# SyncE fetches one of the 64 row tiles of a round, row by row

## The reference

```python
f0, f1 = fctp_scalar(x0, x1, node_attr, W_l1_0, W_l1_1, MUL)   # a row of 128 numbers per node
weight = (SILU_NORM * silu(edge_scalars @ (W_fc1 / 8.0))) @ (W_fc2 / 8.0)
g0 = f0[edge_src]                       # 32 numbers of the source's row
g1 = f1[edge_src]                       # 32 x 3 numbers of it
outA = wA * g0 * e0
outB = wB * einsum('euk,ek->eu', g1, e1) / SQRT3
outC = (wC * g0)[..., None] * e1[:, None, :]
outD = wD[..., None] * g1 * e0[..., None]
# mA .. mD: segment sums of these by edge_dst; then small matrices, cos and sin, a layer norm
```

## Time and profile before

| | us |
|---|---|
| median of 3 runs | 7639.68 (7636.81 to 7649.67) |
| the profiled execution | 7641.61 |
| its span | 7639.8 |
| product stage: first to last gather | 3564.9 to 7595.2 |

### The profile page before, as it was taken

The page is one execution under the profiler, slowest core; times in us unless marked ns, Lnnn a source line. Parts: engine busy times, 40 slices in busy tenths (PEclk is TensorE's granted clock), DMA queues, the critical chain, the costliest instruction groups (busy, mean ns, idle before and its releaser), DMA issues.

```text
span 7639.8 us, 124729 instructions
## 1 busy us (share of the span) xinstructions
PE 6634.2 (87%) x37394; PEld 5567.6 (73%) x37395; DVE 4749.6 (62%) x9176; ACT 3358.7 (44%) x6752; POOL 4896.2 (64%) x4864
## 2 busy tenths in 40 slices
PE   6999978999987999986888888888888888888887
PEld 4666656888876888875777777777777777777776
DVE  9999984333334333337666666666666666666665
ACT  5999975555545555544222222222222222222222
POOL 2211104777764777764777777777777777777775
PEclk9999998999989999998787777777777777777777
DMA  3666556555545555546333333333333333333332
GB/s 81 133 132 129 124 121 192 166 165 164 167 126 167 167 166 166 167 132 171 85 86 85 87 85 87 85 86 88 85 86 86 85 87 85 85 87 85 87 87 58
DMA packets 630499, 881.07 MB, mean 115 GB/s; under 512 B 218687, under 2 KB 496670, under 8 KB 625236
## 3 DMA queue, kind: packets, MB, share of 16 engines
q0 software_dynamic: 158000, 437.63, 22.5%
q1 hardware_dynamic: 446192, 427.03, 19.7%
q10 hardware_dynamic: 26036, 12.80, 0.6%
HBM read 713.32 MB, written 163.70 MB: 115 GB/s over the span
## 4 chain that ended last, share of the span: by engine, by line
POOL 34%; issue 13%; DMA 3%; DVE 2%; POOLq 1%; DVEq 0%; SPq 0%; PE 0%; ACT 0%; ACTq 0%
POOL t_rows L1776 34%; DMA t_rows<-table,t_ends 2%; DMA t_attrs<-in_edge_attr 1%; DVE t_msg_ad L1992 1%; POOLq L179 0%; DVE t_msg_bc L2006 0%; DVE t_cg L1991 0%; SPq L1748 0%; DVE t_msg_ad L1994 0%; POOLq L1774 0%; DVE t_ge L1988 0%; DVE t_rel L2079 0%; DVE acc L1969 0%; DVE t_msg_bc L2001 0%; PE t_sums L1913 0%
## 5 line engine op out<-in xcount | busy, mean ns | idle before, releaser
L1776 POOL DMA_INDIRECT t_rows<-table,t_ends x3224 | 3049.1, 946 | 1009.5 <-issue 966.9
L1021 POOL DMA_INDIRECT c_early<-table,c_first_src x1408 | 1563.5, 1110 | 661.1 <-issue 452.8
L1797 ACT ACTIVATE t_weight<-t_weight,t_attrs 128x64 f32<-128x64 f32 x3224 | 694.6, 303 | 2629.2 <-PE t_weight L1877 2611.4
L1913 PEld LDWEIGHTS t_sums<-t_hot,t_msg_ad 128*128 128x128 f32 x6464 | 971.5, 235 | 922.2 <-issue 921.6
L1096 ACT ACTIVATE c_wide_act<-c_raw 128x1024 fp32r<-128x1024 uint8 (+1 forms) x1120 | 1160.0, 1038 | 884.7 <-PE c_sums L1209 881.3
L1913 PE MATMUL t_sums<-t_hot,t_msg_ad 128*128 x6464 | 1002.1, 321 | 619.4 <-DVE t_hot L2086 618.9
L1174 DVE CAST c_wide_dve<-c_raw 128x1024 fp32r<-128x1024 uint8 (+1 forms) x1120 | 653.3, 585 | 1261.7 <-PE c_sums L1209 1259.1
L1209 PE MATMUL c_sums<-c_wide_act,c_parts 128*128 128x512 f32 (+1 forms) x4480 | 1213.1, 393 | 73.7 <-DVE c_parts L1158 63.0
L1988 DVE TENSOR_TENSOR t_ge<-t_rows,t_edge 128x768 f32<-128x768 f32 x403 | 384.6, 954 | 1195.4 <-DMA t_rows<-table,t_ends 1188.0
L1916 PE MATMUL t_sums<-t_hot,t_msg_bc 128*128 x6464 | 1098.9, 342 | 0.0
L1916 PEld LDWEIGHTS t_sums<-t_hot,t_msg_bc 128*128 128x128 f32 x6464 | 1063.3, 257 | 0.0
(11 more groups left out here) (234 smaller groups left out, 6652.1 us busy)
## 6 DMA issues: line engine op xcount, KB each, us to landing
c_raw<-a_dram SPq DMA_DIRECT2D x532, 448.0 KB, 3.5
a_dram<-a_a_sb POOLq DMA_DIRECT2D x39, 3136.0 KB, 18.2
t_scal<-in_edge_attr SPq DMA_DIRECT2D x403, 256.0 KB
t_rows<-table,t_ends POOLq DMA_INDIRECT x3224
c_early<-table,c_first_src POOLq DMA_INDIRECT x1408, 3.2
t_ends<-in_edges SPq DMA_DIRECT2D x403, 8.0 KB
t_attrs<-in_edge_attr SPq DMA_DIRECT2D x403, 16.0 KB
c_raw<-a_dram SPq DMA_DIRECT2D x28, 224.0 KB, 2.5
```

What stands on the lines that cost most here:

```text
L1021: pool.indirect_dma_start(out=rows_of_group[:, q % 2, t], out_offset=None, in_=table_of_rows, in_offset=bass.IndirectOffsetOnAxis(ap=c.fir ...
L1776: pool.indirect_dma_start(out=rows[:, slot, t, :], out_offset=None, in_=table, in_offset=bass.IndirectOffsetOnAxis(ap=ends[:, slot, t:t + ...
L1797: mul = act.activation(ad, ad, ACT.Copy, scale=attrs[:, slot, t, 0:1])
L1913: pe.matmul(sums[:, of, 0:WIDE], msg_ad[:, slot % 2, t, :], hot[:, of, t, :], start=t == 0, stop=t == T - 1)
```

## The change

From round 1 to round 49, the last column of slot 0 (`rows[:, 0, 7, :]`) is no longer gathered by GpSimd. SyncE fetches its 128 rows one by one, each with a transfer of its own whose address comes from a register. The 128 source numbers of a round lie in one row of a new input `picks` (built on the host from the same numbers) and are brought into one partition of SBUF by a transfer at the end of the round before. The 128 rows are split into seven parts of 18 or 19; slots 0 to 6 of the round issue one part each, after their own loads. A part's numbers come into 19 registers by one register load. Each part has a semaphore, and VectorE waits for all seven ahead of the product of slot 0. The counts that SyncE and VectorE wait for on slot 0's gathers go from 8 to 7 a round.

```diff
+PICKED = [range(P * k // 7, P * (k + 1) // 7) for k in range(7)]
+AT_ONCE = 19
...
+        def picked(slot, r):
+            return slot == 0 and (not isinstance(r, int) or 1 <= r < ROUNDS)
+        def gathered(slot, r):
+            if slot > 0:
+                return r * (16 * T) + 16 * T
+            return r * (16 * (T - 1)) + 16 * T + (16 if isinstance(r, int) and r == ROUNDS else 0)
...
+                def load_picks(r):
+                    sp.dma_start(picks_of[:], picks[bass.ds(r, 1), :]).then_inc(picks_landed, 16)
+                def pick_rows(slot, r):
+                    if slot == 0:
+                        due = worked_out(sp, picks_reg, r * 16)
+                        sp.wait_ge(picks_landed, 16)
+                        sp.wait_ge(picks_landed, due)
+                    if slot < len(PICKED):
+                        for k, p in enumerate(PICKED[slot]):
+                            if k % AT_ONCE == 0:
+                                few = min(AT_ONCE, PICKED[slot].stop - p)
+                                sp.load(some[0:few], picks_of[0:1, p:p + few])
+                            row = sp.snap(some[k % AT_ONCE], min_val=0, max_val=N - 1)
+                            sp.dma_start(rows[p:p + 1, 0, T - 1, :], table[bass.ds(row, 1), :]
+                                         ).then_inc(picked_landed[slot], 16)
...
-                        landed = worked_out(sp, landed_reg, r * (16 * T))
+                        landed = worked_out(sp, landed_reg, gathered(slot, r - 1))
...
                     if i is not None and slot == 6:
                         load_nodes(i, i, FULL)
+                    if picked(0, r):
+                        pick_rows(slot, r)
+                    if slot == SLOTS - 1:
+                        load_picks(r + 1)
...
-                    for t in range(T):
+                    for t in range(T - 1 if picked(slot, r) else T):
                         pool.indirect_dma_start(
...
-                    dve.wait_ge(rows_landed[slot], r * (16 * T) + 16 * T)
+                    dve.wait_ge(rows_landed[slot], gathered(slot, r))
+                    if picked(slot, r):
+                        for k, some in enumerate(PICKED):
+                            dve.wait_ge(picked_landed[k], r * (16 * len(some)))
```

More of the change, by code:

```diff
@@ L1623, in _, with product_edges @@
                 staged_steps(dve, [residual, normalise])
-def product_edges(nc, c, table, edges, attr, scalars, acc, x1_dram, skip_dram, out_dram, bounds_dram):
+def product_edges(nc, c, table, edges, picks, attr, scalars, acc, x1_dram, skip_dram, out_dram, bounds_dram):
     ctx = ExitStack()
@@ L1673, in product_edges @@
         in_time = sb("in_time", [P, 1])
+        picks_of = sb("picks", [1, P], I32)
         sums = ps("sums", (P, 2, 512))
@@ L1682, in product_edges @@
         rows_landed = [sem(f"rows_landed{i}") for i in range(SLOTS)]
+        picks_landed = sem("picks_landed")
+        picked_landed = [sem(f"picked_landed{k}") for k in range(len(PICKED))]
         groups_past, cleared, rel_ready, hot_ready, sums_ready, sums_added = [
@@ L1724, in _ @@
                 past_reg, landed_reg = sp.alloc_register("t_sp_past"), sp.alloc_register("t_sp_landed")
+                picks_reg = sp.alloc_register("t_sp_picks")
+                some = [sp.alloc_register(f"t_sp_pick{i}") for i in range(AT_ONCE)]
+                def load_picks(r):
[13 more added lines that the diff above has]
+                                         ).then_inc(picked_landed[slot], 16)
                 sp.dma_start(bounds_of[:], bounds_dram.rearrange("(a g) e -> a (g e)", a=1)
@@ L1756, in body @@
                         load_nodes(i, i, FULL)
+                    if picked(0, r):
+                        pick_rows(slot, r)
+                    if slot == SLOTS - 1:
+                        load_picks(r + 1)
                 split_rounds(sp, body)
+                sp.wait_ge(picks_landed, ROUNDS * 16)
                 nth = last_steps(sp, "sp", load_nodes)
@@ L2112, in _, with gnn_kernel @@
                 last_steps(dve, "dve", step)
-def gnn_kernel(nc, x, edges, first_edges, pairs_of_edges, coarse, fine, dst_groups, attr, scalars, node_vec, w, out):
+def gnn_kernel(nc, x, picks, edges, first_edges, pairs_of_edges, coarse, fine, dst_groups, attr, scalars, node_vec, w, out):
     def dram(name, shape, dt=F32):
@@ L2171, in gnn_kernel @@
         with nc.sbuf_tensor("acc_2", [D, 2, NB + 1, P], F32) as acc:
-            product_edges(nc, c, table_2, edges, attr, scalars, acc, x1_dram, skip_dram, out,
+            product_edges(nc, c, table_2, edges, picks, attr, scalars, acc, x1_dram, skip_dram, out,
                           bounds_dram)
@@ L2195 @@
     first_edges = edges[:SG].reshape(SG, P, 2, T).transpose(1, 2, 0, 3).reshape(P, 2 * SG * T)
+    picks = np.concatenate([src_groups[0:ROUNDS * SLOTS:SLOTS, :, T - 1], src_groups[:1, :, T - 1]])
     padded = STEPS * STEP - E
@@ L2215 @@
     edges_d = given("edges", edges)
+    picks_d = given("picks", picks)
     first_d = given("first_edges", first_edges)
@@ L2227 @@
     out = nc.dram_tensor("out_0", [N, D], F32, kind="ExternalOutput").ap()
-    gnn_kernel(nc, x, edges_d, first_d, pairs_d, coarse_d, fine_d, dst_d, attr, scalars, node_vec, w, out)
+    gnn_kernel(nc, x, picks_d, edges_d, first_d, pairs_d, coarse_d, fine_d, dst_d, attr, scalars, node_vec, w, out)
     result = run_bass_kernel_spmd(nc, [arrays], core_ids=[0])
```

## The result

The changed kernel takes 8599.7 us (8593.1 to 8608.8), the kernel before beside it 7641.1 us: a ratio of 1.1256, 95% interval 1.1242 to 1.127. That is 959 us, or 19.6 us for each of the 49 rounds, which now take 99.6 us. The forecast was 7681 us with a range up to 7900 us. The direction was right, the size far off.

What follows compares the result with a forecast made beforehand. GpSimd's gather pace bound the kernel at 80.03 us a round; afterwards SyncE's 73.5, landing 1.35 and VectorE 6.0 make 80.85, adding 40 us over 49 rounds to 7641.6: 7681 us, range 7575 to 7900.

Steps and rivals of the forecast that it cites:

- GpSimd's beat and the gain without SyncE: Product stage: gathers every 1.25 us set the round; one fewer in slot 0 saves 61.3 us over 49 rounds.
- One row: SyncE's one-row transfer: issue plus address from a register, taken as 0.435 us, 55.7 us for 128 rows.
- Rival 2: SyncE's row issues: in a train, a single-partition issue costs as much as a 128-partition one; 7900 to 8215 us, chance 0.12.
- One register load: SyncE's load of 18 or 19 numbers: 0.65 us plus 0.05 of gap, seven a round, 4.9 us.
- rival 3: SyncE's register loads cost by number: 22 us a round more, 102.9 us a round, 8760 us; chance 0.03.
- Slower instead of faster: Whole kernel's direction: slower 0.51, faster 0.35, same 0.14; likeliest single case 7657 to 7835 us, at 0.36.
- my sum: Slot 0's refill cycle: SyncE 73.5 us, landing 1.35, VectorE 6.0; 80.85 us a round.
- The lap: Slot 0's refill: VectorE's count, SyncE's work, landing, VectorE's work back to the count; ends last at 80.85 us against GpSimd's 78.8.
- Landing and VectorE's share: After SyncE's last row: 1.35 us until VectorE starts, then 6.0 us from slot 0's product to VectorE's count.
- 25.15 + 128 x: Slot 0's refill cycle in us, x being one row's time; break even at x = 0.429, full gain to 0.419.
- Edits at nothing: Changes costed at zero: slot 7's load of numbers, late group loads, VectorE's extra waits; covered by waiting or slack.

## Why the prediction was wrong

- **GpSimd's beat and the gain without SyncE**: right. 61 us forecast, 61 measured.
- **One row**: 0.423 us against 0.435; its three parts are the rows that I had put together (44, 29 and 228 ns). Rival 2 is out: in a train, the issues are no dearer than alone.
- **One register load: this step failed.** I took 0.65 us, with 1.30 as the upper end; in the round shown it took 1.59 to 4.13, 23.0 us in all in place of 4.6. I had read a price by number from rows of one, four and eight numbers. In those rows the four and the eight begin at multiples of 16 bytes of their tiles, so by the runs above they are one and two reads, and the step of 254 ns from four to eight is the price of a read, not of four numbers. Alignment is only a part of it: even aligned, a load costs 1.17 to 1.59 us, about twice my price or more, and the run with aligned parts (7933 us) still lies above my range. A row that I had left out would have warned me, the load of two numbers on VectorE in the kernel before, dearer by 200 ns than the load of four:

```profile
L1283 DVEq TENSOR_LOAD <-r_bounds x2: 543/545/547, 2259.2 to 3419.8; - x2
```

- The Trainium skill's sentence (page "Runtime: NRT & Kernel Launch", section "Instruction fetch mechanics"), about 200 ns a register even in bulk, is told there of register loads that the runtime injects; I carried it over to the kernel's own loads from SBUF. Here five of the seven loads agree with it (3.87 us for 18), and aligned ones do not (1.17 us for 16). By the sign that I had set for it, loads near 3.8 us, rival 3 is the case that came nearest; I had given it 0.03 and 8760 us, and 8600 was measured.
- **Slower instead of faster**: luck, as far as my sum goes. With the measured 0.423 us for a row and my own price of the load, the lap is 25.15 + 54.1 = 79.3 us, less than the 80.03 of before, and the forecast would have been faster by some 36 us. The dear loads made it slower.
- **The lap** as a mechanism: right in place and form, though only the wait of 1.6 us in it hangs on VectorE; SyncE's own 98.0 us would have been too long without it. With the measured loads and rows in my sum it is 80.85 + 18.4 - 1.5 = 97.7 us against 99.6. Landing and VectorE's share were right to 0.1 us. Of the 1.9 us that are missing, some 1.4 are four pauses of 0.3 to 0.4 us in SyncE's stream. One is seen above: t_scal ends at 5495.24 and t_ends starts at 5495.83, 0.59 us, where 0.25 us is usual. Two lie in trains of rows (in the round from 5001 they take 7.80 us for 18 rows and 8.22 for 19, where 7.43 and 7.85 are usual), and one behind the third train (0.66 us to t_scal, where 0.36 is usual). I had called the mechanism wrong if the round exceeds 25.15 + 128 x, here 79.3 us, by over 2 us. It exceeds it by 20.3, but that line held my price of the load fixed; the round with one load shows that it was the size.
- **Edits at nothing**: slot 7's issues, the branch and the load of the numbers were to take some 3 us and took 5.7, since the way back of SyncE's loop became longer (last section). So the wait in slot 0, which was to be some 5 us, was 1.6; they stayed covered.

## What to carry to other kernels

Price a register load by its reads, not by its numbers: let every load begin at a multiple of 16 bytes (here of its tile, whose own place in SBUF no run varied) and hold a multiple of four numbers. Here 4 bytes decided over 902 us. Before a price by size is taken from two rows, look whether both have the same alignment, and use the row that does not fit. Where an engine refills a buffer in place, lay its work, the landing and the reader's work end to end and compare that lap with the round of the bottleneck; an engine that waits three fifths of its time, as SyncE did before, can still be the one that ends last.

## What was not expected of the hardware

The loop of SyncE became long, and its instructions seem to be fetched anew in each pass. The page's row of queue q14, before and after (packets, MB, share):

```profile
q14 instruction: 101, 0.83, 0.0%
```
```profile
q14 instruction: 386, 3.16, 0.1%
```

The 285 packets more are six for each of the loop's 46 passes, and a few (an estimate from these counts; the longer program alone would be fetched once). All kernels here with one-row issues in SyncE's loop have 386 to 389 of these packets, the one with seven gathers and no rows 102.

At the end of a round the next instruction comes late: the last issue of slot 7 ends at 5079.50 and t_scal starts at 5082.75, 3.25 us. The kernel before needs 0.67 us (5014.01 to 5014.68), the one with seven gathers and no rows 0.71. First the changed kernel, then the one before:

```profile
5079.25 0.25 SPq L1744 DMA_DIRECT2D t_picks<-in_picks  x1
5082.75 0.34 SPq L1778 DMA_DIRECT2D t_scal<-in_edge_attr  x1
5084.65 0.33 SPq L1783 DMA_DIRECT2D t_ends<-in_edges  x1
```
```profile
5013.68 0.33 SPq L1752 DMA_DIRECT2D t_attrs<-in_edge_attr  x1
5014.68 0.33 SPq L1743 DMA_DIRECT2D t_scal<-in_edge_attr  x1
```

The pause stands behind the loop's branch: in the changed kernel the branch starts at 5079.6 and the next register operation at 5082.3, in the kernel before at 5014.1 and 5014.3. That the packets and the pauses belong together is argued; the run without the rows lost the packets and the long way back, and no run took one away and kept the other.
